# Query turns moved from TensorE to VectorE and DRAM, with the orders of all engines rewritten, in a four-stage decoder kernel

## The reference

```python
q = einsum('bsd,ed->bse', x, Wq)         # 8 batches x 128 tokens, 32 heads of 128
k, v = x @ Wk.T, x @ Wv.T                # 8 key heads
q, k = rope(rmsnorm(q)), rope(rmsnorm(k))
k_all = concat(k_cache[block_table], k)  # 512 cached + 128 new keys
scores = where(valid, q @ k_all.T * SCALE, -1e30)
out = (softmax(scores) @ v_all) @ Wo.T
```

## Time and profile before

| what | value |
|---|---|
| median of 3 runs | 1328.07 us (1327.75 to 1328.84) |
| profiled execution | 1327.64 us |
| its span of instructions | 1325.9 us |
| mean granted TensorE clock | 0.999 |
| TensorE busy | 1302.4 us (98%) |
| VectorE busy | 1037.4 us (78%) |
| ScalarE, POOL busy | 843.8, 844.0 us (64% each) |

### The profile page before, as it was taken

The page is one execution under the profiler, slowest core; times in us unless marked ns, Lnnn a source line. Parts: engine busy times, 40 slices in busy tenths (PEclk is TensorE's granted clock), DMA queues, the critical chain, the costliest instruction groups (busy, mean ns, idle before and its releaser), DMA issues.

```text
span 1325.9 us, 25249 instructions
## 1 busy us (share of the span) xinstructions
PE 1302.4 (98%) x7316; PEld 1135.4 (86%) x7316; DVE 1037.4 (78%) x2235; ACT 843.8 (64%) x2217; POOL 844.0 (64%) x1116
## 2 busy tenths in 40 slices
PE   9898999999999999999999999999999899999999
PEld 8787888888888888888888888888888688888887
DVE  7977887888787878787888788778888886748546
ACT  7566666766676656666766676666666774635444
POOL 7677777777777767777777786777766832415111
PEclk9999999999999999999999999999999999999999
DMA  5578658745874687468547844884554453454542
GB/s 204 193 212 270 151 143 230 243 127 158 228 215 130 177 238 196 130 183 259 143 127 221 270 110 127 231 274 107 190 132 114 133 171 129 138 177 154 181 140 80
DMA packets 215388, 233.14 MB, mean 176 GB/s; under 512 B 134817, under 2 KB 174369, under 8 KB 204577
## 3 DMA queue, kind: packets, MB, share of 16 engines
q1 hardware_dynamic: 209568, 196.24, 51.0%
q0 software_dynamic: 5760, 36.18, 8.6%
HBM read 166.31 MB, written 66.06 MB: 175 GB/s over the span
## 4 chain that ended last, share of the span: by engine, by line
PE 88%; DVE 8%; POOL 2%; issue 1%; ACT 1%; DMA 1%; SPq 0%; DVEq 0%; POOLq 0%; ACTq 0%
PE ps L65 26%; PE ps L66 25%; PE ps L67 25%; PE ps L1245 5%; DVE at_scores L984 2%; DVE at_pT_lo L932 2%; PE ps L1227 2%; DVE shared L1452 1%; PE ps L2196 1%; PE ps L1287 1%; DMA at_pT_raw<-turned_rows 1%; PE ps L1221 0%; DVE at_turned L1011 0%; POOL at_probs L565 0%; PE ps L2229 0%
## 5 line engine op out<-in xcount | busy, mean ns | idle before, releaser
L730 ACT ACTIVATE at_probs<-at_scores,at_neg_max 128x640 f32<-128x640 f32 x256 | 211.4, 826 | 250.7 <-DVE at_neg_max L984 250.3
L565 POOL TENSOR_SCALAR at_probs<-at_probs,at_row_inv 128x640 f32<-128x640 f32 x256 | 223.1, 876 | 129.7 <-DVE at_row_inv L990 128.5
L984 DVE CUSTOM_DVE_ANT_0 at_scores<-ps,at_mask,at_inv_rms 128x640 f32<-128x640 f32 x256 | 220.3, 879 | 30.8 <-PE ps L67 29.0
L65 PE MATMUL ps<-ds_hi,x_hi 128*128 128x512 f32 (+1 forms) x564 | 198.5, 352 | 0.8 <-DVE x_lo L1502 0.4
L67 PE MATMUL ps<-ds_hi,x_lo 128*128 128x512 f32 (+1 forms) x564 | 192.5, 341 | 0.0
L65 PE MATMUL ps<-at_kT_hi,ds_lo 128*128 128x320 f32 x512 | 159.2, 311 | 9.4 <-DVE at_neg_max L984 6.7
L67 PE MATMUL ps<-at_kT_hi,ds_lo 128*128 128x320 f32 x512 | 158.8, 310 | 0.0
L66 PE MATMUL ps<-at_kT_lo,ds_lo 128*128 128x320 f32 x512 | 158.7, 310 | 0.0
L932 DVE TENSOR_TENSOR at_pT_lo<-ps,at_pT_hi 128x512 fp32r<-128x512 f32 x196 | 133.8, 684 | 7.0
L65 PE MATMUL ps<-at_pT_hi,at_v_hi 128*128 128x512 f32 x320 | 129.6, 405 | 6.6 <-DVE at_pT_lo L932 6.1
L66 PE MATMUL ps<-at_pT_lo,at_v_hi 128*128 128x512 f32 x320 | 126.5, 395 | 0.0
(11 more groups left out here) (221 smaller groups left out, 3592.7 us busy)
## 6 DMA issues: line engine op xcount, KB each, us to landing
turned_rows<-at_turned SPq DMA_DIRECT2D x62, 512.0 KB
at_pT_raw<-turned_rows SPq DMA_DIRECT2D x248, 128.0 KB
kT_pages<-shared SPq DMA_DIRECT2D x16, 1024.0 KB
kv_raw<-kT_pages SPq DMA_DIRECT2D x60, 256.0 KB, 5.4
v_pages<-shared SPq DMA_DIRECT2D x14, 1024.0 KB
kv_raw<-v_pages SPq DMA_DIRECT2D x56, 256.0 KB, 4.7
sw_wgu_raw<-in_sw_gu SPq DMA_DIRECT2D x22, 512.0 KB, 3.4
staging<-in_L_cond_Wo SPq DMA_DIRECT2D x8, 1024.0 KB, 5.1
```

The costliest lines, as they stand in the source:

```text
L65: pe.matmul(out, l_hi, r_hi, start=first, stop=False)
L565: pool.tensor_scalar(probs[:, h, :], probs[:, h, :], row_inv[:, h:h + 1], 1.0, ALU.mult, ALU.mult).then_inc(probs_done, 1)
L730: act.activation(probs[:, h, :], scores[h % 2][:], ACT.Exp, bias=neg_max[:, h:h + 1], scale=-1.0, accum_out=row_sum[:, h:h + 1]).then_inc( ...
L984: dve.tensor_tensor_reduce(out=scores[h % 2][:], in0=slot(h), in1=mask[:, b, :], scale=inv_rms[b % 2][:, h:h + 1], scalar=3.0e38, op0=ALU. ...
```

## The change

The queries of all items but the first two are no longer turned by TensorE. VectorE turns them in blocks of 32x32 (`spread_queries`, one operation over 128x512), SyncE stores them to a DRAM tensor `q_rows` in four DMAs and reads them back in one, and ScalarE and VectorE split them from the SBUF copy `qT_raw`.

With it the orders change. TensorE starts the round with the query product, now waiting only for the squares of the round before; the key turn directly follows the probabilities' turns, and the output product comes after it. The first product with V waits for VectorE's sum of the output (`y_added`), and the second moves behind score 3. VectorE does the queries' low part and `turn_q` early, the sum of the output later, one reciprocal for heads 0 and 1, and one turn for heads 0 to 2 of the probabilities; it takes the weight subtraction n = 2 from POOL, and its subtractions of Wo move behind the masks. ScalarE squares the queries before the exponentials, which work in place in `probs` (the `scores` buffers are gone). POOL rotates the queries earlier, and its page gather comes after that; tables for item b + 3 are made in round b. SyncE reads the queries first, loads the keys, stores the turned probabilities, stores a page (in groups 1 to 6 this is now one round later by number, and ahead of the values), loads the values, reads the turned probabilities back and stores the queries. Some semaphores are shared or renamed.

```diff
+            def store_queries(g, b):
+                wait_apart(sp, q_spread, upto(g, b, 1, 1) - 2, passed)
+                for a in range(NQ):
+                    sp.dma_start(q_rows.rearrange("(k i) (a n) -> a i k n", k=NQ, a=NQ)[a],
+                                 q_turned_rows[a * SQ:(a + 1) * SQ].rearrange("i k h r -> i k (h r)")).then_inc(q_moved, 16)
+            def read_queries(g, b):
+                wait_apart(sp, q_moved, q_moves(g, b, NQ), passed)
+                sp.dma_start(qT_raw[:].rearrange("p a h r -> p (a h r)"), q_rows).then_inc(q_moved, 16)
...
@@ SyncE, a round
-                    if by_moves(g, b):
-                        move_turned(g, b)
+                    if not (last and b == B - 1) and q_by_moves(g1, b1):
+                        read_queries(g1, b1)
...
                         wait_apart(sp, kc_done, upto(g, b, 1, 1), passed)
+                        load_keys(g2, b2)
+                    if by_moves(g, b):
+                        store_turned(g, b)
+                    if not by_row(g) and not last and 2 <= b < 6:
+                        store_pages(g, b - 2)
+                    if not (last and b >= B - 2) and not by_row(g2):
                         wait_apart(sp, v_cache_done, upto(g, b, 1, 1), passed)
-                        load_keys(g2, b2)
                         load_values(g2, b2)
+                    if by_moves(g, b):
+                        read_turned(g, b)
...
+                    if not (last and b >= B - 2):
+                        store_queries(g2, b2)
...
-                    elif not last and 1 <= b < 5:
-                        store_pages(g, b - 1)
...
@@ VectorE
+            def two_inverses(g, b):
+                dve.wait_ge(exp_done, upto(g, b, G, 2))
+                dve.reciprocal(row_inv[:, 0:2], row_sum[:, 0:2]).then_inc(inv_done, 2)
+            def turn_first_heads(g, b, n):
+                dve.wait_ge(probs_done, upto(g, b, G, n))
+                dve.transpose(turned[:, :, :, 0:n, :].rearrange("p k c h r -> p h c k r"),
+                              probs[:, 0:n, (KC - MOVED) * P:KEYS].rearrange("p h (c k i) -> p h c k i", c=MOVED, k=NQ)).then_inc(turned_done, n)
+            def spread_queries(g, b):
+                dve.wait_ge(q_rot_done, upto(g, b, 1, 1))
+                dve.transpose(q_turned_rows[:].rearrange("p k h r -> p h k r"),
+                              q_rot[:].rearrange("p h (k i) -> p h k i", k=NQ)).then_inc(q_spread, 1)
...
@@ TensorE
-                    pe.wait_ge(qT_done, upto(g, b, 1))
+                    if by_row(g) and b == 2:
+                        pe.wait_ge(qT_done, 2)
+                    else:
+                        pe.wait_ge(q_squared, upto(g, b, 1, 1))
...
+                    if started:
+                        project_q(g2, b2, range(DC))
...
                     probs_T_part(g, b)
-                    queries(g1, b1)
+                    if not started:
+                        queries(g1, b1)
                     probs_T_rest(g, b)
-                    if started:
-                        output(*preceding(g, b))
                     new_keys(g1, b1)
...
+                        output(*preceding(g, b))
...
                     if by_moves(g, b):
+                        pe.wait_ge(*((dense.x1_ready, b) if last and b else (y_added, upto(g, b, 1))))
                         times_v(g, b, 0)
-                        times_v(g, b, 1)
                     score(g1, b1, 2)
                     score(g1, b1, 3)
+                    if by_moves(g, b):
+                        times_v(g, b, 1)
```

More of the change, by code:

```diff
@@ L596, in group, with stage @@
                     started = not (first and b == 0)
-                    if first and b == 0:
+                    def stage():
+                        if first and 2 <= b < 6:
+                            stage_pages(g, b - 2)
+                        if not first and not last and 1 <= b < 5:
+                            stage_pages(g, b - 1)
+                    if not started:
+                        key_scale(g2, b2)
                         stage_first_keys(0)
+                    if b == B - 3 and not last:
+                        qkv_group(g + 1, DC)
                     if keys_by_row(g2, b2):
@@ L814, in group @@
                             probs_T(g, b, c)
+                    if b == B - 3 and not last:
+                        qkv_group(g + 1, 0)
+                    squares(g2, b2)
                     if b == 0:
@@ L822, in group @@
                     if b == B - 3 and not last:
-                        for n in (DC, DC + 1, *range(DC)):
+                        for n in range(1, DC):
                             qkv_group(g + 1, n)
@@ L1068, in group @@
                         attended(*preceding(g, b))
-                    if b == 1:
-                        wo_group(g, 3)
-                    if b == B - 2 and not last:
-                        qkv_group(g + 1, 1)
-                    queries(g1, b1)
+                        new_values(g1, b1)
+                        queries(g1, b1)
+                        turn_q(g2, b2, 0)
+                        turn_q(g2, b2, 1)
+                    else:
+                        queries(g1, b1)
+                    probs_T(g, b, 0)
@@ L1098, in group @@
[L1098 to L1099 removed]
+                        turn_k(g2, b2)
+                    if b == B - 3 and not last:
+                        qkv_group(g + 1, 0)
                     if started:
[L1101 to L1102 removed]
+                        spread_queries(g2, b2)
+                        add_y(*preceding(g, b), last and b > 0)
                     mask_and_max(g1, b1, 0)
@@ L1111, in group @@
+                    if last and b in EFF_FIRST:
+                        dense.weights(dve, *EFF_FIRST[b])
                     if b == B - 3 and not last:
-                        qkv_group(g + 1, 0)
-                    mask_and_max(g1, b1, 2)
-                    inverse(g1, b1, 1)
+                        qkv_group(g + 1, 1)
                     mask_and_max(g1, b1, 3)
@@ L1117, in group @@
                         probs_T(g, b, 3)
+                        probs_T(g, b, 4)
+                    if b == 0:
+                        wo_group(g, 2)
+                        wo_group(g, 3)
+                    if last and b in EFF_SECOND:
+                        dense.weights(dve, *EFF_SECOND[b])
+                    if b == B - 3 and not last:
+                        qkv_group(g + 1, 2)
                     inverse(g1, b1, 2)
-                    if by_moves(g, b):
-                        probs_T(g, b, 4)
-                    if last and b in EFF_BEFORE_INVERSE:
-                        dense.weights(dve, *EFF_BEFORE_INVERSE[b])
+                    if first and b == 0:
+                        angle_turns(late_sin, late_cos, slice(EARLY, B))
+                    if first and b == 1:
+                        angle_reduce(late_sin, late_cos)
                     inverse(g1, b1, 3)
-                    if by_moves(g1, b1):
-                        for h in range(G):
-                            turn_squares(g1, b1, h)
+                    turn_first_heads(g1, b1, G - 1)
+                    if first and b == 1:
+                        angle_ends(late_sin, late_sin, late_cos)
+                    turn_squares(g1, b1, G - 1)
             def ending(g):
@@ L1742, in load_w3 @@
                 sp.dma_start(w3_raw(i), weight[bass.ds(a, 1)].rearrange("o p k d -> p (o k) d")).then_inc(w3_loaded[W3_RAW[i]], 16)
+            for b in range(QUAD, B):
+                loads.pick(sp, b)
             sp.wait_ge(dense.sums_done, 2)
```

232 lines of the change are left out of this document (121 added, 111 removed).

## The result

The changed kernel takes 1371.22 us (median of 4 runs, 1370.04 to 1377.87), beside 1328.12 us for the kernel before in the same comparison: ratio 1.0334, 95% interval 1.0301 to 1.0368. It is 43 us slower. The prediction was 1302 us, range 1290 to 1323, with 0.11 for slower. It was wrong in size and in sign. The profiled execution has a span of 1369.2 us (before 1325.9), and a mean granted TensorE clock of 0.989 (before 0.999).

The account below looks back on a forecast made before the run. The prediction took TensorE's own work, 15.84 us a round, as the bound. Its sum was 1327.64 - 26.7 + 8.4 - 5.0 - 2.8 = 1301.5, stated as 1302 us because the profiled execution lay 0.4 below the median; range 1290 to 1323.

Parts of the forecast that it names:

- Query turns off TensorE: TensorE, 62 of 64 rounds: four query turns of 0.43 us per round go, saving 26.7 us.
- Spread: VectorE's one new 128x512 query turn per round, taken at 0.77 us, bounds 0.43 and 0.85.
- VectorE's order: VectorE within a plain round: its results meet TensorE's deadlines with 0.2 to 0.4 us to spare.
- Rival (b): VectorE's middle becomes the bound: y and mask 0 late by 0.3 us in 62 rounds, 1321 us, chance 0.15.
- Rounds b = 5: VectorE's weight subtractions and ScalarE's conversions delay spread and y: 1.2 us lost in seven groups, 8.4 us; bounds 0 and 1.8.
- DMAs: SyncE's extra stores and reads stay hidden; turned probabilities land by T+10 to 11 after the query product starts; no cost.
- rival (a): SyncE's queue, some 31 page-staging rounds: reads of turned probabilities land late; 1348 us at 1.5 us each, chance 0.11.
- the limit for the landing: Turned probabilities may land as late as 11.9 us after the query product's start at no cost.
- First group: Waits for POOL's tables and VectorE's angles end there: 5.0 us taken back of 11.2 idle, bounds 0 and 10.
- Waits that end: Other groups: TensorE's weight loads no longer wait for probabilities' low part behind a Wo subtraction; 2.8 us saved, bounds 0 and 2.8.

Follow-up runs that it names:

- e10: e7 with the next group's weights loaded in three 0.5 MB parts in b = 0, 1 and 2, not one piece in b = 1: 1320.55 us.
- e2: Changed kernel with the next group's weights loaded behind the reads of turned probabilities, still in b = 4: 1387.54 us.
- e5: e1 with the next group's 1.5 MB of weights loaded in one piece in b = 1, behind the reads of turned probabilities: 1353.37 us.
- e7: e5 and e6 together: 1343.37 us, ratio 1.0105.
- e6: e3 with ScalarE's repeated waits for the next weights also taken out, 369 recorded instructions per iteration: 1359.84 us.
- b1: Kernel before the change with two already fulfilled waits per round added to ScalarE's loop, 383 recorded instructions: 1335.50 us, ratio 1.0052.
- e1: Changed kernel with POOL subtracting weight chunk 1 instead of 3 in b = 5, and VectorE chunk 3 instead of 1: 1348.31 us.
- e9: e10 with weight parts in b = 1, 2, 3, and the first group's page stores one round later, behind the queries' read: 1330.00 us.
- e3: Changed kernel without two already fulfilled waits per round in ScalarE's loop, 377 recorded instructions for 392: 1372.74 us.

## Why the prediction was wrong

*Query turns off TensorE, 26.7 us.* Right. The plain rounds are 15.28 to 15.48 us where 15.4 was said; per round about 0.43 was gained. The last group gained 6.4 us in seven rounds.

*Spread.* 699 ns against 0.77 taken. VectorE's busy time grew by 25.5 us (1062.9 less 1037.4), 0.41 us for each of 62 rounds, where 0.8 was put on it. VectorE's order held in the plain rounds: TensorE waited 3.4 us in all for y in the loop. Rival (b) did not happen.

*Rounds b = 5: +8.4 us.* The step that failed most. I counted VectorE's three subtractions, and not what waits for them: I had said that POOL's normalising gets easier, and nothing of POOL's own part n = 3, which waits for the last of them with four normalisations behind it. Priced at 1.2 us a group, this place cost far more: b = 5 and 6 lost 4.0 + 0.4 against before, and against a plain round of 15.33 4.5 + 0.9. With that wait gone the term was 1.8 (17.12, e10), at the upper bound that I gave.

*DMAs: nothing for the order on SyncE.* The second failed step: the term was put at nothing. What came is rival (a), with a chance of 0.11, whose place and releaser were right, and whose count was not: 31 rounds were named, only b = 4, with the weights ahead, is hit in the loop. There it is 3.0 us a group, of which moving the weights off brings back 2.1 to 2.4 (e2, e5). The page store alone (b = 2 and 3) did not pass the limit for the landing in the changed kernel; in e10, b = 4 is 0.65 us above a plain round with nothing but it ahead of the reads. For the queries I worked out a slack of 3 us in a plain round and did not ask what a large load in front would do with it; e7 showed 9.1 us.

*Jump back of the loop.* The third failed step: it is in no term of the sum and in no rival. It was 13 us by e6; b1 shows the same cause in the kernel before, at 6.1 us.

*First group: -5.0.* It was +10.7, with the clock at 0.92 for 0.99, up to 8.8 us of it by the estimate above. Some 2.9 are place 2 (e1). Even e10 is 4.9 us above before. ScalarE waits there for both reads, in a queue that also carries tokens, x and four page stores; in e9 turning the order of two of them only moved the wait. Which wait costs how much there, and what order would be free, is open.

*Waits that end, 2.8 us.* It did not come: in the loop the weight loads' waits for the low part of probabilities grew from 2.8 to 31.4 us.

The sum in the loop, by the runs: about +13 from place 3, +22 from place 2, +13 to 14 from the weights of place 1 (6 x 2.1 to 2.4), together 48 to 49. From 800.4 that leaves about 752, and e10, with all three mended, measured 754.3. The mended change gains 9.0 us in the loop and 4.9 in the last group, loses 4.9 in the first and 2.9 at start and end: 6.1, or but for rounding the 6.2 of span between 1325.9 and 1319.7. So the forecast's main term was sound, and in the loop the three places cost 48 to 49 us beside it.

## What to carry to other kernels

Before an instruction that shares a counting semaphore with another engine is moved, list what stands behind it on its own engine: the wait costs what the queue behind it costs. On a queue where a store has a dependent read, look for the largest transfer ahead of either, in every round and not only in the typical one; cut bulk loads to what fits in the idle stretch. And count each engine's instructions per loop iteration: waits and register steps are code, and where the loop no longer stays loaded the jump back charges for it.

## What was not expected of the hardware

A hardware loop of 368 or 369 recorded ScalarE instructions ran with no code fetched inside it; 377, 383 and 392 brought 22 or 23 packets in about five iterations, and 1.7 to 4.3 us of idle time behind the branch. In the changed kernel it is a step between 369 and 377: e3 took out 15 of the 24 added instructions and gained nothing, and e6 8 more and gained 13 us in the loop.

A stall can be paid again in clock, but is not each time. Behind 2.6 to 3.3 us of idle time in round b = 5 of the changed kernel, one of six rounds b = 6 ran at 0.90 granted and took 16.90 us; the other five ran at 1.00 and took 16.06 or 16.07. In e2, where TensorE idled some 6 us in each round b = 5 (25.13 us with 19.13 busy in one of them), the clock fell to 0.86 to 0.93 within that round in all six groups.
